# Four sequences instead of two in the loop of each engine: expert MLP, layer norm and rotation over 128 sequences

## The chip, the cores and the metric

The kernel runs on one core of one Trainium2 chip. Its time is the device time of one execution in microseconds (us). The core's engines each run a program of their own, and meet at semaphores: TensorE (PE in the profile; PEld is its loading of weights), VectorE (DVE), ScalarE (ACT), GpSimd (POOL) and SyncE (SP). DMA queues move data between memory and the core, and also bring the engines their instructions.

## The reference

There are 128 sequences of 128 tokens with 512 features. Each sequence names one of 8 experts; that expert's two-layer network, a residual, a layer norm and a rotation of groups of four features by the sequence's own two angles give the output.

```python
h = jax.nn.gelu(jnp.einsum('bsh,bhi->bsi', input_tensor, Wi_b) + bi_b[:, None, :], approximate=False)
o = jnp.einsum('bsi,bih->bsh', h, Wo_b) + bo_b[:, None, :]
r = o + input_tensor
mu = jnp.mean(r, axis=-1, keepdims=True)
var = jnp.mean(jnp.square(r - mu), axis=-1, keepdims=True)
y = (r - mu) * jax.lax.rsqrt(var + LN_EPS)
...
x0, x1, x2, x3 = (e[..., 0], e[..., 1], e[..., 2], e[..., 3])
out = jnp.stack([x0 * ct + x1 * st, -x0 * st + x1 * ct, x2 * cp + x3 * sp, -x2 * sp + x3 * cp], axis=-1)
```

Here `Wi_b`, `bi_b` and the others are the expert's arrays picked for each sequence, (512, 2048) and (2048, 512) for the two products; y is scaled by gamma and shifted by beta before the rotation, and ct, st, cp, sp are the cosines and sines of the sequence's theta and phi.

## The kernel before, in words

The sequences are sorted by expert at the start, on the chip; a table `tab` in SBUF says for each place s in that order which sequence it is, the rank of its expert among those used, and which of two weight buffers holds that expert. Weights and activations are split into a high and a low f16 part, and a product is made of three f16 products (`PASSES`), so that each of the two matrix products takes 4 groups (one for each PSUM bank of 512 columns) of 12 matmuls of 128x128 by 512 columns: 96 matmuls for a sequence.

All engines walk through the same places s. In its iteration s TensorE alternates between a group of the first product of s (`first_product`, L834, into `z_ps`) and a group of the second product of s-1 (`second_product`, L850, into `o_ps`). VectorE scales and adds the bias (`z_bank`, L647), ScalarE takes the gelu and the high part, VectorE takes the low part (`lo_group`, L657), SP transposes both parts by DMA into `hT16` (L257), which the second product of the next iteration reads. VectorE also prepares the input of s+1 (`scale_x`, `lo_x`) and does the residual, the layer norm and the rotation of s-2. GpSimd loads and splits the weights of the next expert, written out for each of the seven later experts and not in a loop. The places of a DMA queue and the order on each engine are the order in which the code is written.

What the change touches is `pipeline`. It gives each of TensorE, VectorE, ScalarE and SP the same schedule: iterations 1 and 2 written out, a loop on the engine itself (`Fori`) whose body holds two iterations and runs for i = 1 to 61 (s = 3 to 124), and the last five (s = 125 to 129, of which the last two only finish earlier sequences) written out. Inside the loop s is a number in a register. At the start of an iteration TensorE reads four entries of `tab` into registers (`slot_value`, L196, an instruction TENSOR_LOAD each, with register arithmetic), checks its semaphores, and only then passes on the first matmul; register and branch instructions run on the engine's sequencer, ahead of the matmuls that it has queued.

Of the kernel before, what the change touches and what calls it, by code (L numbers as in the profile page):

```python
# [67 lines left out]
def expert_mlp_rotate_kernel(nc, x, itok, theta, phi, Wi, bi, Wo, bo, gamma, beta, out):  # L68
    S, T, H = x.shape
# [11 lines left out]
    with ctx:  # L81
# [116 lines left out]
        def pipeline(engine, iteration):  # L198


            iteration(1, 1)
            iteration(2, 0)
            with engine.Fori(1, (S - 4) // 2) as i:
                iteration(i * 2 + 1, 1, True)
                iteration(i * 2 + 2, 0, True)
            for s in range(S - 3, S + 2):
                iteration(s, s % 2)

        def there(s, d, inner):
# [22 lines left out]
        def _(sp):  # L232
# [36 lines left out]
            iteration(-1, 1)  # L269
            iteration(0, 0)  # L270
            pipeline(sp, iteration)


# [165 lines left out]
        def _(act):  # L439
# [120 lines left out]
            hi_parts(1)  # L560

            pipeline(act, iteration)
            store(S - 1)
            act.wait_ge(s_y, 16 * S)
# [3 lines left out]
        def _(dve):  # L568
# [227 lines left out]
            lo_parts(1)  # L796

            pipeline(dve, iteration)


# [111 lines left out]
```

## Time and profile before

| | us |
|---|---|
| three runs | 2800.49, 2804.8, 2823.32 |
| their median | 2804.8 |
| the profiled execution: its time | 2803.09 |
| its span, first to last instruction | 2801.4 |
| TensorE busy in the span | 2684.1 |

The profiled execution lies 1.7 us below the median of the three, and its span 1.7 us below its own time. The granted clock of TensorE is 0.991 of full speed over the span.

### The profile page before, as it was taken

The page shows a single profiled execution, that of the slowest core. Times are in us where ns is not written, and L with a number is a line of the kernel's source. Part 1 is how long each engine was busy: PE and PEld are TensorE (multiplying, and loading weights), DVE is VectorE, ACT ScalarE, POOL GpSimd, SP SyncE. Part 2 cuts the span into 40 slices and gives each one's busy share as a digit, 9 for nine tenths or more (in the row PEclk, how much of TensorE's full clock was granted, in tenths as well). Part 3 has the DMA queues.
Part 4 walks back from the last instruction along what each step waited for, and adds up shares of the span by engine and source line. Part 5 has one row for each costly group of instructions (what it writes and reads, how often), then busy time and mean ns, then how long its engine had stood idle before and what let it go on. Part 6 is the DMA issues. An engine that isn't in the chain of part 4 may idle for free.

```text
span 2801.4 us, 55611 instructions
## 1 busy us (share of the span) xinstructions
PE 2684.1 (96%) x12306; PEld 1208.4 (43%) x12307; DVE 1956.2 (70%) x4919; ACT 931.1 (33%) x1689; POOL 1369.6 (49%) x1619
## 2 busy tenths in 40 slices
PE   2899999999999999999999999999999999999998
PEld 1344444444444444444444444444444444444443
DVE  4576677667777767777777776777777776777676
ACT  4333333333333333333333333333333333333332
POOL 4778617871007872478600478606873577500000
PEclk9899999999999999999999999999999999999999
DMA  4658556765436665657544658546675658444343
GB/s 159 150 132 195 118 136 148 182 144 122 86 82 167 173 148 126 147 130 186 139 98 88 147 131 180 141 98 157 159 162 132 165 131 168 113 91 89 82 97 65
DMA packets 742561, 375.90 MB, mean 134 GB/s; under 512 B 682816, under 2 KB 682944, under 8 KB 733824
## 3 DMA queue, kind: packets, MB, share of 16 engines
q1 hardware_dynamic: 677568, 173.95, 34.9%
q0 software_dynamic: 25984, 130.29, 14.7%
q10 hardware_dynamic: 38976, 71.32, 7.8%
q14 instruction: 25, 0.20, 0.0%
q8 instruction: 8, 0.13, 0.0%
HBM read 174.13 MB, written 33.55 MB: 74 GB/s over the span
## 4 chain that ended last, share of the span: by engine, by line
PE 78%; DMA 6%; DVE 6%; issue 5%; DVEq 2%; POOL 2%; ACT 1%; ACTq 0%; SPq 0%; POOLq 0%
PE z_ps L834 39%; PE o_ps L850 39%; DMA xT<-x 3%; DMA hT<-h 2%; DVE z_ps L647 1%; DVEq L196 1%; DMA xbuf<-in_x 1%; ACT z_ps L472 1%; DVE h L657 0%; ACT x L467 0%; DVE y L702 0%; POOL wo L340 0%; ACTq L196 0%; DVE ln L674 0%; DVE r_ps L673 0%
## 5 line engine op out<-in xcount | busy, mean ns | idle before, releaser
L834 PE MATMUL z_ps<-wi,xT 128*128 x6096 | 1407.2, 381 | 45.0 <-issue 21.7
L850 PE MATMUL o_ps<-wo,hT 128*128 x6144 | 1415.7, 380 | 17.2 <-DMA hT<-h 9.2
L834 PEld LDWEIGHTS z_ps<-wi,xT 128*128 128x128 f16 x6096 | 598.0, 98 | 781.4 <-issue 89.0
L850 PEld LDWEIGHTS o_ps<-wo,hT 128*128 128x128 f16 x6144 | 602.6, 98 | 748.4 <-issue 29.0
L472 ACT ACTIVATE z_ps<-z_ps 128x512 f32<-128x512 f32 x512 | 299.3, 585 | 1777.7 <-DVE z_ps L647 1763.4
L647 DVE SCALAR_TENSOR_TENSOR z_ps<-z_ps,tok,bi_all 128x512 f32<-128x512 f32 x512 | 387.5, 757 | 203.6 <-PE z_ps L834 144.5
L406 POOL TENSOR_TENSOR wi<-staged 128x512 f32<-128x512 f32 x112 | 117.1, 1046 | 658.3 <-DVE r_ps L667 647.2
L657 DVE SCALAR_TENSOR_TENSOR h<-z_ps,tok,h 128x512 f16<-128x512 f32 x512 | 380.6, 743 | 2.5 <-ACT h L478 1.6
L478 ACT ACTIVATE h<-z_ps,tok 128x512 f16<-128x512 f32 x512 | 352.4, 688 | 21.9 <-DMA hT<-h 0.4
L652 DVE SCALAR_TENSOR_TENSOR x<-xbuf,tok,x 128x512 f16<-128x512 f16 (+1 forms) x128 | 115.7, 904 | 192.2 <-ACT x L467 192.2
L702 DVE SCALAR_TENSOR_TENSOR y<-r_ps,rot,y 128x128 f32<-128x128 f32 x512 | 194.5, 455 | 5.8 <-ACT y L485 2.6
L339 POOL TENSOR_SCALAR staged<-staged,wscale 128x512 f32<-128x512 f32 x224 | 158.4, 707 | 20.9
L340 POOL TENSOR_TENSOR wo<-staged,wo 128x512 f16<-128x512 f32 x112 | 130.7, 1167 | 9.3
L340 POOL TENSOR_TENSOR wi<-staged,wi 128x512 f16<-128x512 f32 x112 | 130.0, 1160 | 9.3
L666 DVE TENSOR_SCALAR ln<-inv,ex 128x1 f32 (+1 forms) x128 | 27.4, 214 | 148.1 <-issue 140.7
L406 POOL TENSOR_TENSOR wo<-staged 128x512 f32<-128x512 f32 x112 | 117.3, 1047 | 7.4
L485 ACT ACTIVATE y<-r_ps,rot 128x256 f32<-128x256 f32 x256 | 109.4, 487 | 17.0 <-DVE r_ps L693 17.0
L408 POOL TENSOR_TENSOR wi<-wi 128x512 f32<-128x512 f32 x84 | 108.6, 1293 | 6.6
L408 POOL TENSOR_TENSOR wo<-wo 128x512 f32<-128x512 f32 x84 | 108.5, 1291 | 6.6
L667 DVE SCALAR_TENSOR_TENSOR r_ps<-o_ps,ln,xbuf 128x512 f32<-128x512 f32 x128 | 97.1, 759 | 19.2 <-DVE ln L666 18.8
L693 DVE SCALAR_TENSOR_TENSOR r_ps<-r_ps,ln,bgb_all 128x512 f32<-128x512 f32 x128 | 97.2, 759 | 18.3
L691 DVE SCALAR_TENSOR_TENSOR r_ps<-r_ps,ln,bgb_all 128x512 f32<-128x512 f32 x128 | 97.1, 759 | 18.2
(126 smaller groups left out, 1407.8 us busy)
## 6 DMA issues: line engine op xcount, KB each, us to landing
staged<-in_L_cond_Wi POOLq DMA_DIRECT2D x56, 1024.0 KB, 5.9
staged<-in_L_cond_Wo POOLq DMA_DIRECT2D x56, 1024.0 KB, 6.7
xbuf<-in_x ACTq DMA_DIRECT2D x128, 256.0 KB, 3.6
out<-y ACTq DMA_DIRECT2D x128, 256.0 KB, 3.4
hT<-h SPq DMA_TRANSPOSE x512, 3.9
bi_all<-in_L_cond_bi POOLq DMA_DIRECT2D x7, 1024.0 KB, 9.4
wi<-in_L_cond_Wi SPq DMA_DIRECT2D x4, 1024.0 KB, 8.5
wo<-in_L_cond_Wo ACTq DMA_DIRECT2D x4, 1024.0 KB, 11.5
```

Of the source, the lines that this page charges most:

```text
L339: chain.step(g.tensor_scalar(raw, raw, scale, 1.0, ALU.mult, ALU.mult))
L340: chain.step(g.tensor_tensor(lo, raw, hi, ALU.subtract))
L406: chain.step(g.tensor_tensor(to, raw[:, p], raw[:, p], ALU.mult))
L408: chain.step(g.tensor_tensor(acc[:, p], acc[:, p], sq[:, p], ALU.add))
L472: a.activation(bank, bank, ACT.Gelu).then_inc(s_gelu, 1)
L478: a.activation(h16[:, n, 0, :], bank, ACT.Copy, scale=HSCALE[k]).then_inc(s_hhi, 1)
L647: v.scalar_tensor_tensor(out=z_ps[:, n, :], in0=z_ps[:, n, :], scalar=ZS, in1=row(bi_all, b, hb), op0=ALU.mult, op1=ALU.add).then_inc(s_z, 1)
L652: v.scalar_tensor_tensor(out=x16[:, 1, :], in0=row(xbuf, s % XB), scalar=SX, in1=x16[:, 0, :], op0=ALU.mult, op1=ALU.subtract).then_inc(s_ ...
L657: v.scalar_tensor_tensor(out=h16[:, n, 1, :], in0=z_ps[:, n, :], scalar=HSCALE[k], in1=h16[:, n, 0, :], op0=ALU.mult, op1=ALU.subtract).th ...
L702: last = v.scalar_tensor_tensor(out=every(y[:], to), in0=every(r_ps[:], of), scalar=row(rot, s, slice(sine, sine + 1)), in1=every(y[:], to ...
L834: last = t.matmul(z_ps[:, n, :], xT16[:, j, a, k, :], wi16[:, bass.ds(b, 1), w, k, cs], start=(k == 0 and (a, w) == PASSES[0]), stop=(k == ...
L850: last = t.matmul(o_ps[:, j, :], hT16[:, n, a, c, :], wo16[:, bass.ds(b, 1), w, n * GC + c, :], start=(n == 0 and c == 0 and (a, w) == PAS ...
```

## The change

The loop's body holds four iterations instead of two and runs 30 times (s = 3 to 122); seven iterations (s = 123 to 129) are written out behind it instead of five. The first two iterations, the work of each iteration and the start of the kernel stay as they are. GpSimd's program is the same instruction by instruction.

```diff
             iteration(1, 1)
             iteration(2, 0)
-            with engine.Fori(1, (S - 4) // 2) as i:
-                iteration(i * 2 + 1, 1, True)
-                iteration(i * 2 + 2, 0, True)
-            for s in range(S - 3, S + 2):
+            with engine.Fori(0, (S - 8) // 4) as i:
+                for j in range(4):
+                    iteration(i * 4 + (3 + j), (1 + j) % 2, True)
+            for s in range(3 + (S - 8) // 4 * 4, S + 2):
                 iteration(s, s % 2)
```

On TensorE, behind the second iteration of the body, the kernel before has the loop's counter and its branch (L203). The branch goes back to the body's first TENSOR_LOAD; what is listed behind it is the first iteration after the loop.

```order
L850 ISA
L850 MATMUL o_ps<-wo,hT 128x512 x2
L203 REGISTER_ALU
L203 COMPARE_AND_BRANCH
L196 TENSOR_LOAD tab
L196 ISA x2
```

At the same place the changed kernel goes on with the third iteration's table reads.

```order
L850 ISA
L850 MATMUL o_ps<-wo,hT 128x512 x2
L196 TENSOR_LOAD tab
L196 ISA x2
L196 TENSOR_LOAD tab
L196 ISA x3
```

So the counter and the branch stand here no longer; they come once behind the fourth iteration. The listing of TensorE's program grows from 1058 rows to 1620.

On VectorE the same place in the kernel before is behind the last instruction of the rotation (L702); L64 clears the semaphore of VectorE's own steps.

```order
L702 SCALAR_TENSOR_TENSOR y<-r_ps,rot,y 128x128
L203 REGISTER_ALU
L203 COMPARE_AND_BRANCH
L64 ISA
L196 TENSOR_LOAD tab
L196 ISA x2
```

In the changed kernel:

```order
L702 SCALAR_TENSOR_TENSOR y<-r_ps,rot,y 128x128
L64 ISA
L196 ISA
L196 TENSOR_LOAD tab
L196 ISA x3
```

Here too the branch has moved behind the fourth iteration. VectorE's listing grows from 551 rows to 821, SP's from 105 to 145, GpSimd's stays at 1696.

## Rows read from the trace of the kernel before

**Rows 1.** The page, part 1: busy time of the engines.
```profile
PE 2684.1 (96%) x12306; PEld 1208.4 (43%) x12307; DVE 1956.2 (70%) x4919; ACT 931.1 (33%) x1689; POOL 1369.6 (49%) x1619
```

**Rows 2.** Chain that ended last, 2500 to 2640: start, us, what.
```profile
2507.62 0.21 issue
2507.83 2.76 PE z_ps L834 x12
...
2528.72 2.59 PE z_ps L834 x12
...
2549.44 0.21 issue
2549.65 2.76 PE z_ps L834 x12
```

**Rows 3.** The same chain in the written-out end, 2690 to 2802.
```profile
2716.75 2.59 PE z_ps L834 x12
...
2737.47 2.59 PE z_ps L834 x12
```

**Rows 4.** Waits of PE: total us, times, longest.
```profile
PE z_ps L834 <- issue: 21.7, 45, 2.7
PE z_ps L834 <- DMA xT<-x: 21.2, 6, 14.3
...
PE o_ps L850 <- DMA hT<-h: 9.2, 6, 3.4
```

**Rows 5.** The chain: the five long pieces of "issue" before PE, 255 to 2337.
```profile
255.85 2.54 issue
...
979.11 2.58 issue
...
1719.70 2.29 issue
...
2038.24 2.15 issue
...
2336.23 2.71 issue
```

**Rows 6.** All DMA queues, 200 to 2700: packets, MB, share of 16 engines.
```profile
q1 hardware_dynamic: 623040, 154.74, 35.4%
q0 software_dynamic: 24890, 122.25, 15.5%
q10 hardware_dynamic: 33984, 61.88, 7.7%
q14 instruction: 14, 0.11, 0.0%
```

**Rows 7.** DMA queue q8, 100 to 200, then 2717 to 2779.
```profile
q8 instruction: 4, 0.07, 0.3%
...
q8 instruction: 3, 0.05, 0.3%
```

**Rows 8.** Windows: 2717 to 2779: length, busy time of PE, PEld, DVE, ACT, POOL.
```profile
2717.00:2779.00 62.00, 62.00 (x289) 28.12 (x288) 43.01 (x111) 19.33 (x35) 0.00 (x0) 1.00 0.39 77
```

**Rows 9.** Timeline of DVE, 2569 to 2613: start, us, what, idle time before.
```profile
2588.82 0.76 DVE L647 SCALAR_TENSOR_TENSOR z_ps<-z_ps,tok,bi_all 128x512 f32<-128x512 f32 x1 [1.31 <-PE z_ps L834]
...
2596.82 0.74 DVE L657 SCALAR_TENSOR_TENSOR h<-z_ps,tok,h 128x512 f16<-128x512 f32 x1
...
2609.93 0.76 DVE L647 SCALAR_TENSOR_TENSOR z_ps<-z_ps,tok,bi_all 128x512 f32<-128x512 f32 x1 [1.58 <-PE z_ps L834]
```

**Rows 10.** The chain, 2300 to 2345: a wait at a change of expert.
```profile
2321.91 11.43 DMA hT<-h
...
2333.47 2.76 PE o_ps L850 x12
```

**Rows 11.** DMA issues: KB each, us from issue to landing.
```profile
hT<-in_itok_B SPq DMA_DIRECT2D x1, 64.0 KB, 3.1
...
hT<-in_condB_phi SPq DMA_DIRECT2D x1, 0.5 KB, 2.6
```

## The prediction

> **What bounds the kernel now.** I read the page's busy times first: TensorE is busy for 2684.1 of 2801.4 us, VectorE for 70% of the span, the others for half or less [rows 1]. So the question is what stands between TensorE's matmuls. The chain that ended last answers it in a quiet stretch, where no weights are being loaded: it is all TensorE, groups of 12 matmuls at 2.59 us, and a sequence of eight groups takes 8 x 2.59 = 20.72 us. Between the first and the second sequence of a loop body nothing is seen: from 2507.83 to the second sequence's first group at 2528.72 are 20.89 us, the eight groups and 0.17 us by which the first group (2.76) is longer than the rest. Behind the second sequence, where the loop jumps back, there are 0.21 us of "issue", and then again a first group of 2.76 [rows 2]. A pair takes 2549.65 - 2507.83 = 41.82 us against 2 x 20.72 = 41.44. In the written-out end of the program, which has no jump, the first groups lie 2737.47 - 2716.75 = 20.72 us apart and are no longer than the others [rows 3]. So a jump back costs TensorE 0.21 + 0.17 = 0.38 us, and a boundary that is written out costs nothing.
>
> The waits of TensorE say how often: 45 first-product instructions waited for "issue", 21.7 us in total [rows 4]. Five of these are long, 12.3 us together [rows 5]; they stand behind waits for a transposed activation, as at 2336.23, where the group before it had waited for a transpose of 11.43 us [rows 10]. The other 40 make 9.4 us, 0.24 each. With the 0.17 of the first group that is 0.41 us. The loop before jumps back 60 times (61 passes), so a third of the jumps cost nothing that shows: TensorE's sequencer was far enough ahead, or something else ended later.
>
> **The change part by part.** The loop of 30 passes jumps back 29 times, so 31 jumps go. Each removed jump becomes a boundary like the one inside the body before: the same four table reads, without counter and branch.
>
> If the removed jumps cost what the average one does, the gain is 31 x 40/60 x 0.41 = 8.5 us. A jump behind a drained queue costs too, though it is not among the 40: counting sequences along the chain, four of the five long pieces stand at jumps, 2.54, 2.58, 2.71 and 2.15, and one, 2.29, between the two sequences of a body [rows 5], so the jump adds some 0.3 there (2.15 ended in another kind of wait and is left out). Counting these four with the others, 31 x 44/60 x 0.41 = 9.3 us. That is the value I take. The upper bound is 31 x 0.41 = 12.7 us, if each removed jump costs what it does in a quiet stretch. The lower bound of this step is nothing, if TensorE then waits for the next in line: transposes of the activations.
>
> What is next in line in a quiet stretch? VectorE waits for TensorE once in each sequence, 1.31 and 1.58 us, before the fourth bank; the low part that closes a sequence is done at 2596.82 + 0.74 = 2597.56 [rows 9], and the group that needs its transpose is the last of the sequence in hand, which by the pattern of [rows 2] starts at 2549.65 + 41.82 + 20.89 - 2.59 = 2609.77. That is 12 us, of which the transpose takes some. So VectorE, ScalarE and SP follow a TensorE that is 0.2 us a sequence faster. Their own 31 jumps go as well, and are worth nothing, since none of them is on the path there.
>
> At changes of expert the weights that GpSimd fetches lengthen the transposes. There TensorE waits: 9.2 us for `hT`, 21.2 for `xT`, of which one wait of 14.3 is at the start [rows 4], and the 12.3 us of long pieces: 9.2 + 6.9 + 12.3 = 28 us in all. The change leaves these transfers and the order of the queues as they are, but shifts when they meet. I price that at nothing, with a quarter of the 28, 7 us, to either side.
>
> Written out in addition are two sequences at the end (123 and 124), with numbers known beforehand instead of registers: by [rows 3] these run at 20.72, which is nothing added. The two longest programs grow by half, and this is where the price could be: **the instructions must reach the engines.** Queue q8 brings them in packets of 0.05 / 3 = 17 KB. It brought three of them in the 62 us from 2717 to 2779, in which TensorE ran three written-out sequences [rows 7, 8]: about one packet for a sequence, and none of them stopped TensorE, which was busy all 62 us. I take q8 for TensorE's. From 100 to 200, when the sequences ahead of the loop and its first passes ran, came four [rows 7]; then, from 200 to 2700, not one [rows 6]. So a body of two sequences, some two to three packets, stays with the engine once loaded, and jumping back to its start asks for nothing. The other instruction queue, q14, serves the others in smaller packets (0.11 / 14 = 8 KB); its 14 packets in that stretch are two for each of the seven experts in GpSimd's written-out code, so VectorE's and ScalarE's bodies stay too. Whether a body of four sequences stays, four to five packets on TensorE, no row shows. From one side it costs nothing; from the other, a transfer at each of 29 jumps while the sequencer stands still. The nearest rows for one transfer's time are the small loads, 2.6 and 3.1 us from issue to landing [rows 11]; 29 x 2.6 to 3.1 is 75 to 90 us. Inside the body the fetch runs ahead, as in the written-out end, so the jump alone would pay. I take nothing, the side of [rows 6], which are the only ones that show jumps back over more code than one packet.
>
> The Trainium skill has a price for the jump itself: "Advanced Engine Details and Errata", section Control Flow Timing, gives about 108 ns for a compare-and-branch. By it 31 jumps would be an estimate of 3.3 us and the time 2800. The trace has more, since the table reads behind the jump come later too and the queue of matmuls runs dry.
>
> **The sum.** 2803.1 (the profiled execution) - 9.3 = 2793.8 us; the median of the three runs lies 1.7 above that execution. I predict 2794 us. The bounds: 2803.1 - 12.7 - 7 = 2783 and 2803.1 + 7 = 2810.
>
> **The rivals.**
>
> *TensorE's body no longer stays with the engine.* Each of 29 jumps waits for a packet with nothing in reserve, since the sequencer comes late there already [rows 2]: 75 to 90 us, less the 9.3, gives 2869 to 2884 us, slower by 2.4 to 2.9%. It decides from the point where the body of four and the packet fetched ahead of it exceed what the engine holds. For it speaks that only two sequences are shown to stay; against it that these stayed for 2500 us without a single packet, so that the store is not just two packets deep. The Trainium skill, "Runtime: NRT & Kernel Launch", section Instruction fetch mechanics, has a rule that makes this case: instructions lie in two blocks, and a taken branch to a target outside them waits for a fetch. By that rule the loop before should have fetched at its jumps as well, which [rows 6] do not show; the same section gives TensorE's store as 2048 instructions, in which the four sequences would fit.
>
> *VectorE's body no longer stays, TensorE's does.* VectorE then starts every fourth sequence some 3 us late. In quiet stretches the 12 us above, less a transpose, hide it. At changes of expert, where transposes take 11 us [rows 10], nothing hides it: the 6 + 6 waits and five long pieces [rows 4, 5] are some 12 places, and if half of them feel 3 us, 18 us come back: 2794 to 2812 us, no difference that can be told.
>
> *The whole path speeds up.* For 1% or more, 28 us, all jumps and most waits at the changes of expert would have to go; by a lucky shift of the transfers this gives 2775 us at best. Nothing in the profile points there.
>
> That the loop is not what it says can be left out: the listing shows the branch behind the fourth sequence.
>
> **How the numbers follow.** About 1% is what a measurement of this kernel can tell from no change. The forecast, 2783 to 2803, has 0.68; VectorE's late start, or the transfers meeting worse, 2803 to 2812, 0.15; TensorE's refetch, about 2876, 0.13; the large gain 0.04. The range 2784 to 2811 holds the first two less their ends, 8 in 10. Faster by over 1%: 0.04. Slower by over 1%: 0.14, the refetch and 0.01 for changes of expert that go badly wrong. Within 1%: 0.82.
>
> **What would show it.** In quiet stretches four sequences should take 4 x 20.72 + 0.38 = 83.26 us, with one piece of "issue" where there were two; waits of TensorE for "issue" should number some 25 instead of 45. Queue q8 should again bring nothing from 200 to 2700, and six or so packets in place of four before that. I am wrong if q8 shows tens of packets and pieces of "issue" of 2 to 3 us stand at each fourth sequence; if q14 does so without q8, the second rival holds; and if the pieces of "issue" are fewer and the time is no shorter, TensorE's waits for `hT` and `xT` have taken the gain.

## The result and the profile after

The changed kernel takes 2789.2 us (median of 20 runs, 2775.2 to 2801.9), the one before in runs beside it 2806.4 (20 runs, 2793.7 to 2823.3). The ratio, with its 95% interval, is 0.9938 [0.9923, 0.9954]: 17 us less, between 13 and 22. Predicted were 2794 us and a gain of 9.3. The range held, the size of the gain did not: nearly twice as much, and the experiments below show that TensorE's own jumps, from which the 9.3 were worked out, carry the smaller part of it.

The profiled execution took 2791.90 us. First the page's busy times, which answer to [rows 1]:

```profile
PE 2679.8 (96%) x12306; PEld 1208.7 (43%) x12307; DVE 1959.2 (70%) x4919; ACT 930.0 (33%) x1689; POOL 1368.4 (49%) x1619
```

TensorE does the same matmuls and is busy 4.3 us less. Most of it can be first groups that are no longer stretched: 21 waits for "issue" fewer (below) at 0.17 us make an estimate of 3.6. Next the chain that ended last, 2490 to 2640 (start, us, what), against [rows 2]:

```profile
2497.45 0.30 issue
2497.74 2.76 PE z_ps L834 x12
...
2580.80 0.27 issue
2581.07 2.76 PE z_ps L834 x12
```

Four sequences take 2581.07 - 2497.74 = 83.33 us, with one piece of "issue" in front (predicted: 83.26). TensorE's waits (us in all, times, longest), against [rows 4]; `xT` is the transposed input that the first product needs, `hT` the transposed activation of the second:

```profile
PE z_ps L834 <- DMA xT<-x: 18.8, 6, 13.9
PE o_ps L850 <- DMA hT<-h: 15.7, 6, 4.9
...
PE z_ps L834 <- issue: 11.5, 24, 2.5
```

"Issue" went from 45 waits to 24, from 21.7 us to 11.5. `xT` is shorter by 2.4 us, but `hT` took 6.5 more. And the queues that bring instructions, 100 to 200 and then 210 to 2660 (packets, MB, share of 16 engines), against [rows 6, 7]:

```profile
q8 instruction: 5, 0.08, 0.4%
```

```profile
q1 hardware_dynamic: 613028, 152.25, 36.8%
q0 software_dynamic: 24832, 121.91, 15.7%
q10 hardware_dynamic: 33552, 61.09, 8.0%
q14 instruction: 14, 0.11, 0.0%
```

Nothing from q8 in the loop: the body of four sequences stays with TensorE, and neither of the refetch rivals happened.

So the signs that were foretold are there, with five packets of q8 from 100 to 200 us in place of four, where six or so had been expected. Is the step behind them right too? In this pair of executions "issue" gave back 10.2 us and TensorE's busy time 4.3, more than 9.3, and then 6.5 were lost on `hT`. If the other engines followed TensorE as the prediction had it, `hT` should not have grown.

### The profile page after: what moved, and what is told of

Same layout as the page of the kernel before. It is cut to its first block, busy times and chain, and to the rows that moved or that the text cites. A ratio compares the mean times of both kernels' runs of the same rounds, so it can differ in the third digit from the quotient of the medians.

```text
span 2790.2 us, 54938 instructions
## 1 busy us (share of the span) xinstructions
PE 2679.8 (96%) x12306; PEld 1208.7 (43%) x12307; DVE 1959.2 (70%) x4919; ACT 930.0 (33%) x1689; POOL 1368.4 (49%) x1619
## 4 chain that ended last, share of the span: by engine, by line
PE 79%; DMA 6%; DVE 5%; issue 4%; POOL 2%; DVEq 2%; ACT 1%; ACTq 0%; SPq 0%; POOLq 0%
PE o_ps L850 40%; PE z_ps L834 39%; DMA hT<-h 2%; DMA xT<-x 2%; DMA xbuf<-in_x 2%; DVE z_ps L647 1%; DVEq L196 1%; ACT z_ps L472 1%; DVE h L657 0%; ACT x L467 0%; DVE ln L674 0%; DVE y L702 0%; DVE r_ps L673 0%; ACTq L196 0%; POOL wo L340 0%
## 5 line engine op out<-in xcount | busy, mean ns | idle before, releaser
L850 PE MATMUL o_ps<-wo,hT 128*128 x6144 | 1419.7, 381 | 24.0 <-DMA hT<-h 15.7
L702 DVE SCALAR_TENSOR_TENSOR y<-r_ps,rot,y 128x128 f32<-128x128 f32 x512 | 195.2, 456 | 5.0 <-ACT y L485 2.0
L667 DVE SCALAR_TENSOR_TENSOR r_ps<-o_ps,ln,xbuf 128x512 f32<-128x512 f32 x128 | 97.1, 759 | 15.4 <-DVE ln L666 13.9
```

What stands on the lines that cost most here:

```text
L702: last = v.scalar_tensor_tensor(out=every(y[:], to), in0=every(r_ps[:], of), scalar=row(rot, s, slice(sine, sine + 1)), in1=every(y[:], to ...
L850: last = t.matmul(o_ps[:, j, :], hT16[:, n, a, c, :], wo16[:, bass.ds(b, 1), w, n * GC + c, :], start=(n == 0 and c == 0 and (a, w) == PAS ...
```

## The experiments

Two theories. **A**, the prediction's: TensorE's jumps are the gain, the others' jumps are hidden. **D**: VectorE's own cycle is hardly shorter than TensorE's. When something at a change of expert has made it late, it catches up slowly or not at all, until a transpose of what it finished late stops TensorE; what its iteration costs in jumps and table reads then counts. In the expectations B is D's forerunner (the jumps of VectorE and ScalarE make the chain late at changes of expert), C says that the transfers there only happen to meet otherwise, and E that ScalarE's or SP's jump is the late one. All gains and losses below are the ratio to the kernel before, run beside, with its 95% interval, times that kernel's median (2801 to 2807 us).

**One engine's loop at a time.** `pipeline` gets a number of sequences for each engine:

```diff
+        BODY = {'sp': 2, 'act': 2, 'dve': 2, 'pe': 4}
...
-            with engine.Fori(1, (S - 4) // 2) as i:
-                iteration(i * 2 + 1, 1, True)
-                iteration(i * 2 + 2, 0, True)
-            for s in range(S - 3, S + 2):
+            n = BODY[name]
+            with engine.Fori(0, (S - 8) // n) as i:
+                for j in range(n):
+                    iteration(i * n + (3 + j), (1 + j) % 2, True)
+            for s in range(3 + (S - 8) // n * n, S + 2):
                 iteration(s, s % 2)
```

e1_pe4, four on TensorE alone.

> Only TensorE's loop holds four sequences; VectorE, ScalarE and SP keep two. Theory A (the gain is TensorE's own: its sequencer comes late at its jumps): all of the change's gain, 2789 us where the kernel before has 2806, that is 12 to 22 us faster, and waits of TensorE for issue fall from 45 to about 25. Theory B (the jumps of VectorE and ScalarE made the chain late at changes of expert): a gain of 5 us or less. Theory C (the transfers at changes of expert only happen to meet otherwise): anything between -8 and +8 us in the waits for hT and xT, with the issue part of 9 to 11 us beside it.

Measured: 2800.2 us, ratio 0.9981 [0.9966, 0.9996], a gain of 5 us (1 to 10). TensorE's waits in it:

```profile
PE o_ps L852 <- DMA hT<-h: 19.9, 9, 4.3
...
PE z_ps L836 <- issue: 15.8, 23, 2.8
```

Half the jumps are gone, as in the changed kernel (23 waits for "issue"), but `hT` takes 19.9 us instead of 9.2. Two thirds of the gain are missing.

e2_rest4, four on SP, ScalarE and VectorE, two on TensorE.

> The other half: VectorE, ScalarE and SP hold four sequences, TensorE keeps two. Theory A: no change, within 4 us of the kernel before, and 45 waits for issue again. Theory B: most of the 17 us. If both halves gain some 8 us each, the two theories share it.

Measured: 2792.5 us, ratio 0.9960 [0.9939, 0.9980], a gain of 11 us (6 to 17). Theory A had nothing for this.

```profile
PE z_ps L836 <- issue: 17.9, 42, 2.7
...
PE o_ps L852 <- DMA hT<-h: 4.6, 2, 2.6
```

TensorE's jumps are all there (42 waits), and the gain comes nonetheless, with two waits for `hT` instead of six. The two parts add up to the whole: 5 + 11 = 16 of 17 us. Theory A had 12 to 22 us for the first and nothing for the second, and falls.

**TensorE's gaps taken away without the loop.** e3_late_reads: the kernel before, but TensorE reads the two table entries that only the second product needs after it has passed on the first group of the first product, so that the sequencer is not late behind a jump.

```diff
-                if back:
-                    b1 = slot_value(pe, BUF, s - 1, 1)
-                    if not boot:
-                        r1 = slot_value(pe, RANK, s - 1, E - 1)
...
                     if here:
                         first_product(s, k, n, b)
+                    if n == 0 and back:
+                        b1 = slot_value(pe, BUF, s - 1, 1)
+                        if not boot:
+                            r1 = slot_value(pe, RANK, s - 1, E - 1)
```

> All loops hold two sequences as before. In TensorE's iteration the two table reads that only the second product needs are moved behind the first group of matmuls, so the sequencer has two reads (some 1.5 us) less to do between the last group of one sequence and the first of the next. Theory A: the jumps then cost nothing, 60 of them instead of the 31 that the change removes, so at least the change's 17 us and up to 35; pieces of issue of 0.2 us vanish, and those of 2.1 to 2.7 us behind a drained queue shrink by some 1.5 us. Theories B and C: no more than 5 us, since no jump is removed.

Measured: 2803.8 us, ratio 1.0002 [0.9983, 1.0021]: nothing (a gain of 5 to a loss of 6), where theory A had 17 us at least. Its waits:

```profile
PE o_ps L850 <- DMA hT<-h: 32.3, 13, 5.0
...
PE z_ps L834 <- issue: 1.4, 3, 0.6
```

The "issue" is gone, 20.3 us of it, and 23.1 us more of `hT` stand in its place: 13 waits instead of 6. This is the clearest case of a gain given back. That TensorE runs faster between the transposes and so meets the next one earlier is how I read it; the trace shows that VectorE is late more often, as counted below.

**VectorE's side.** Where the path leaves TensorE in the kernel before, it runs through VectorE for whole sequences; the chain that ended last, 1330 to 1440 (a wider stretch than any shown so far; DVEq is VectorE's sequencer, L196 the table read):

```profile
1341.32 0.70 DVEq L196
...
1347.03 0.77 DVE z_ps L647
...
1362.85 0.30 DVEq L196
...
1368.10 0.77 DVE z_ps L647
...
1383.37 0.73 DVEq L196
...
1389.11 0.77 DVE z_ps L647
...
1392.82 11.75 DMA xT<-x
1404.56 0.33 issue
1404.89 2.76 PE z_ps L834 x12
```

The first z bank of three sequences in a row lies on the chain: VectorE needs 1389.11 - 1347.03 = 42.08 us for two sequences, where TensorE needs 41.82 with a jump and 41.44 without one. Here it doesn't catch up; the input that it prepares late goes through its transpose, and TensorE waits. No matmul of TensorE lies on the chain in these 42.08 us: 26.4 are VectorE and its sequencer, 6.4 ScalarE and its sequencer, whose results VectorE waits for, and 9.3 "issue". So what is called VectorE's cycle is an iteration of VectorE with the steps of ScalarE inside it.

e5_dve4 has four on VectorE alone, e6_act4 on ScalarE alone (`dve` or `act` 4 in the `BODY` line of the first diff, 2 for the others).

> Only VectorE's loop holds four sequences, the others two. Theory D (VectorE, once a transfer has made it late, runs a cycle hardly shorter than TensorE's, so what its jumps take is what it lacks to catch up, and TensorE pays later in waits for transposes): most of the 14 us that the three engines together gave, that is 7 to 14 us faster than before, with waits for issue as before (about 45). Theory E (ScalarE's or SP's jump is the late one): 3 us or less.

> Only ScalarE's loop holds four sequences. Theory D: 0 to 4 us faster. Theory E: 7 us or more.

Measured: VectorE 2799.5 us, ratio 0.9969 [0.9948, 0.9989], a gain of 9 us (3 to 15). ScalarE 2799.8 us, ratio 0.9985 [0.9965, 1.0004], a gain of 4 us, which can't be told from nothing (a loss of 1 to a gain of 10). That is inside what theory D had for both, but the two medians are only 0.4 us apart and the two intervals overlap, so the pair doesn't tell VectorE's loop from ScalarE's. The profiled execution of e5 took 2808.7 us, 9 more than its median, and has 18.6 us of `hT`; its waits say nothing for D, only its time does.

e7_dve_one_read leaves all loops at two and takes away one of VectorE's three table reads in an iteration. The buffer of an expert is its rank modulo 2, so one entry gives both.

```diff
-                    b, r = slot_value(dve, BUF, s, 1), slot_value(dve, RANK, s, E - 1)
+                    r = slot_value(dve, RANK, s, E - 1)
+                    b = r % 2
```

> Loops of two as before. VectorE works out which weight buffer a sequence has from its expert's rank (r % 2, a register operation), and no longer reads it from the table: one read of three less in each of its iterations. No jump goes. Theory D: VectorE's cycle is shorter by some 0.4 us in every sequence, more than its jumps cost (0.26 us in every second), so at least 7 us and up to 25 us faster than before, and fewer sequences in which VectorE starts the first bank over 3.6 us after TensorE finished it (21 in the profile before). Theory A: no change, within 4 us.

Measured: 2794.6 us, ratio 0.9958 [0.9939, 0.9977], a gain of 12 us (6 to 17), with not one jump removed.

```profile
PE z_ps L835 <- issue: 18.2, 50, 3.2
...
PE o_ps L851 <- DMA hT<-h: 0.3, 1, 0.3
```

TensorE's jumps cost about what they did before; its waits for `hT` are gone. The sequences with a late VectorE, counted as in the expectation (first bank begun over 3.6 us after TensorE finished it), are 2 instead of 21.

e9_dve_extra_read goes the other way: the changed kernel, with one more table read in VectorE's iteration, whose value nobody uses.

```diff
                     b, r = slot_value(dve, BUF, s, 1), slot_value(dve, RANK, s, E - 1)
+                    slot_value(dve, RANK, s, E - 1)
```

> The changed kernel with one table read more, of no use, at the start of each of VectorE's iterations (the opposite of the run with one read less). TensorE's program is that of the changed kernel. Theory D: VectorE's cycle is some 0.4 to 0.7 us longer, so the change's gain is lost, 2800 to 2825 us against 2789, and the sequences with a late VectorE are well over the 13 of the changed kernel. Theory A: within 4 us of the changed kernel.

Measured: 2838.8 us, ratio 1.0132 [1.0111, 1.0153] to the kernel before, 37 us slower (31 to 43), and some 50 slower than the changed kernel: more than the 2800 to 2825 us that were expected. 98 sequences have a late VectorE, against 13 in the changed kernel. In e3 they are 34. (These are counts of one execution each; e1 and e6, which leave VectorE's loop alone, have 15 and 9, so a difference of ten or so from 21 says little.) The page's shares of the chain by engine, of before, of the changed kernel, of e7 and of e9 in this order:

```profile
PE 78%; DMA 6%; DVE 6%; issue 5%; DVEq 2%; POOL 2%; ACT 1%; ACTq 0%; SPq 0%; POOLq 0%
```

```profile
PE 79%; DMA 6%; DVE 5%; issue 4%; POOL 2%; DVEq 2%; ACT 1%; ACTq 0%; SPq 0%; POOLq 0%
```

```profile
PE 86%; DMA 4%; issue 3%; DVE 3%; POOL 2%; DVEq 1%; ACT 1%; ACTq 0%; SPq 0%; POOLq 0%
```

```profile
PE 39%; DVE 24%; issue 13%; DVEq 9%; ACT 6%; DMA 5%; POOL 2%; ACTq 1%; SPq 0%; POOLq 0%
```

One table read more in each iteration of VectorE (a load, its address arithmetic and a check of the value), and the chain lies on TensorE for 39% of the span only. In e9's chain, 1430 to 1525, the first z banks of five sequences follow each other:

```profile
1435.93 0.77 DVE z_ps L647
...
1457.43 0.77 DVE z_ps L647
...
1478.47 0.77 DVE z_ps L647
...
1499.43 0.77 DVE z_ps L647
...
1521.22 0.77 DVE z_ps L647
```

Four sequences take VectorE 85.29 us here, against TensorE's 83.33: in this stretch VectorE is the bound. The same row of VectorE's waits for TensorE, before, after, e7 and e9, shows how little lies between these cases:

```profile
DVE z_ps L647 <- PE z_ps L834: 144.5, 114, 3.8
```

```profile
DVE z_ps L647 <- PE z_ps L834: 156.8, 111, 3.8
```

```profile
DVE z_ps L647 <- PE z_ps L835: 183.6, 131, 3.8
```

```profile
DVE z_ps L647 <- PE z_ps L835: 47.4, 41, 3.8
```

VectorE's reserve, its wait for TensorE, is 144.5 us over 128 sequences before, 1.1 us each. In the changed kernel it is there in 111 sequences, with a read more in 41: the read took it for over half of all sequences.

**Both sides at once.** e10_fewer_reads: loops of two, VectorE as in e7, and TensorE reads only the ranks (two reads in an iteration instead of four).

```diff
-                    b1 = slot_value(pe, BUF, s - 1, 1)
-                    if not boot:
+                    if boot:
+                        b1 = slot_value(pe, BUF, s - 1, 1)
+                    else:
                         r1 = slot_value(pe, RANK, s - 1, E - 1)
+                        b1 = r1 % 2
                 if here:
-                    b, r = slot_value(pe, BUF, s, 1), slot_value(pe, RANK, s, E - 1)
+                    r = slot_value(pe, RANK, s, E - 1)
+                    b = r % 2
```

> Loops of two. Both TensorE (two reads instead of four) and VectorE (two instead of three) work out the weight buffer from the rank. TensorE's jumps then cost nothing, as in the run with late reads, which gained nothing by it; VectorE's cycle is that of the run with one read less, which gained 11 us. Theory D: now TensorE's part pays too, since VectorE can follow, 20 to 30 us faster than before, more than the two runs' gains together. If the two parts only add up: 8 to 14 us.

Measured: 2764.1 us, ratio 0.9873 [0.9851, 0.9896], 36 us less (29 to 42), more than the 20 to 30 expected and far more than the 8 to 14 of parts that only add up.

```profile
PE o_ps L851 <- DMA hT<-h: 6.2, 4, 2.6
...
PE z_ps L835 <- issue: 1.8, 3, 0.9
```

TensorE's gaps alone gave 0 (e3), VectorE's read alone 12 (e7); together they give 36. With VectorE on time, what TensorE gains stays. One part of this comparison is not clean: e3 moves TensorE's two reads and e10 drops them, and dropping them on TensorE alone was not run. Of the 43.8 us between the profiled spans of before and e10, 27.0 are waits for "issue", `xT` and `hT`, and 15.7 TensorE's busy time (2668.4 against 2684.1 us), of which more below.

e4_no_loop writes out all iterations on all four engines.

```diff
-            with engine.Fori(1, (S - 4) // 2) as i:
-                iteration(i * 2 + 1, 1, True)
-                iteration(i * 2 + 2, 0, True)
+            for s in range(3, S - 3):
+                iteration(s, s % 2, True)
```

> No loop on any engine: all 130 iterations are written out, with numbers instead of registers; every instruction is fetched once. Theory A with instructions fetched ahead in time: all 60 jumps gone, twice the change's gain, 2765 to 2785 us. If fetching straight code costs TensorE something, time is lost in pieces of issue at every packet of q8: about 140 packets, slower than the kernel before if each costs over 0.2 us.

Measured: 2763.5 us, ratio 0.9843 [0.9813, 0.9873], 44 us less (36 to 52). The instruction queue of TensorE over the whole run:

```profile
q8 instruction: 136, 2.23, 0.3%
```

That is about one packet for a sequence, and "issue" is 1.8 us in one wait, so fetching code that runs straight on costs nothing that shows, as [rows 7, 8] had it. The jumps are not all that is gone: without a register for s the arithmetic on it goes too (the page counts 51151 instructions against 55611), and VectorE's wait for TensorE rises from 144.5 to 245.9 us.

e12_no_loop_fewer_reads joins e4 and e10.

> No loop on any engine, and the fewer reads of both TensorE and VectorE: what the experiments point to. VectorE's cycle without loops is already short enough to follow, so the reads can bring only a little of the 20 us that remain in waits at changes of expert: 2745 to 2765 us, at least as fast as the run with no loop (2763.5).

Measured: 2756.3 us, ratio 0.9847 [0.9821, 0.9873], 43 us less (36 to 50). Not to be told from e4: with "issue" at 0.9 us and `hT` at 2.5 little is left for either edit to give. e4 and e12 are the fastest kernels of the study; e10, with a loop of two, comes close, its interval overlapping both of theirs.

**Where the rivals begin.** e8_all8 has eight sequences in every loop (15 passes), e11_pe8 in TensorE's alone.

> All loops hold eight sequences, 15 passes. By the jumps that go (45 instead of 31) some 20 to 28 us faster than the kernel before, if the eight sequences stay with the engines. If TensorE's body (about nine packets of q8) no longer stays: a burst of q8 packets in every pass, and at each of 14 jumps a wait of 2.6 us or more, 36 us and more lost, so slower than or equal to the kernel before. If only VectorE's body no longer stays: q14 shows tens of packets more, and the time is 2780 to 2800 us.

> Only TensorE's loop holds eight sequences, the others two. If the 58 us that eight sequences on all engines lost are TensorE's fetches at its 14 jumps: slower than before by 50 to 80 us, q8 with some ten packets in each pass and q14 with only the 14 of GpSimd. If VectorE's fetches had a part in it: 30 us or less.

Measured: 2864.3 us, ratio 1.0208 [1.0179, 1.0237], and 2864.4 us, ratio 1.0215 [1.0191, 1.0239]: 58 and 60 us slower. Instruction queues from 200 to 2600, of e8 and then of e11:

```profile
q8 instruction: 152, 2.49, 0.4%
q14 instruction: 180, 1.47, 0.2%
```

```profile
q8 instruction: 152, 2.49, 0.4%
q14 instruction: 14, 0.11, 0.0%
```

And e11's chain at two of its jumps:

```profile
2214.41 3.45 issue
2217.86 2.76 PE z_ps L842 x12
...
2567.80 4.07 issue
2571.86 5.30 PE z_ps L842 x12
2577.16 2.98 PE o_ps L858 x12
```

With eight the first rival is there: 152 packets in 14 passes, eleven for a pass. The second jump costs 4.07 us of "issue", 2.71 in the first group and 0.39 in the next, 7.2 us; the first one costs 3.45 and 0.17. What differs is the granted clock of TensorE, here of the two first groups (start:end, length and busy times as in [rows 8], then the clock, the DMA share and GB/s):

```profile
2217.90:2220.60 2.70, 2.70 (x13) 1.32 (x14) 0.77 (x5) 0.00 (x0) 0.00 (x0) 1.00 0.02 6
2571.86:2577.16 5.30, 5.30 (x13) 2.01 (x14) 1.82 (x7) 0.00 (x0) 0.00 (x0) 0.50 0.02 3
```

Behind the wait of 4.07 us TensorE ran at 0.50, the lower of its two levels (1.2 GHz), behind the one of 3.45 at full speed. At 13 of e11's 14 jumps the first group takes 4.1 us or more. All 14 waits together are 63.9 us, 3.4 to 8.8 each. Of the 65.4 us between the profiled spans of before and e11, "issue" makes 47.8 (69.5 us in 18 waits against 21.7) and TensorE's busy time 15.4 (2699.5 against 2684.1). In e8 "issue" is 79.0 us in 19 waits. The engines on q14 refetch in e8 alone (180 packets against 14), and that costs nothing that shows beside e11: 58 against 60 us. VectorE still waits 191.9 us for TensorE in e8, so there is room to hide it; what the longer loops of these engines would have given stands against it and isn't told apart.

The clock is at work in the kernel before, too; this is the chain at the long piece of [rows 5] that stands between the two sequences of a body:

```profile
1719.70 2.29 issue
1721.99 4.45 PE z_ps L834 x12
```

The granted clock was 0.51 from 1722.00 to 1725.40, and the group took 1.9 us more than 2.59. So a long wait can cost TensorE more than its own length, though not each one does (the 3.45 us in e11 did not), and what decides it isn't shown here. A kernel with few waits, as e10, has few groups at the lower clock and few stretched ones; its TensorE is busy for less.

## Why the prediction was right, and where it was not

**The jump itself** was sized well in a quiet stretch: 83.33 us for four sequences against 83.26, 24 waits for "issue" against about 25. In the whole pair the 10.2 us of waits and 4.3 of busy time are 14.5, above the 9.3 taken and above the upper bound of 12.7, and not all of it is jumps: the long waits for "issue" went from five, 12.8 us together by the idle times of the timeline, to three, 5.9 (2.51, 1.67 and 1.75). The prediction had counted those among the waits at changes of expert. It also left out that TensorE ran at the lower clock behind some of them (a group of 4.45 us behind the 2.29 above), where it had 0.17 for a first group.

**"Their own 31 jumps go as well, and are worth nothing"** is the step that failed. The 12 us between VectorE's last low part and its reader were read in one quiet stretch [rows 9], at a VectorE that was on time. There the reserve is real. In the stretch of 1330 to 1440, where GpSimd works on the next expert's weights (busy for 37.5 of the 42.08 us), VectorE is behind and has no reserve at all, and what decides is not how far its result is ahead of its reader elsewhere but how its cycle compares with TensorE's: 42.08 against 41.82 us, not shorter at all. The other engines' loops were worth 11 us (e2); e5 and e6 don't tell how much of it is VectorE's. So that the measured 2789 us lie inside the range is in part luck: the step that was to give 9.3 us gives about 5 (e1), and the larger part came from a step put at nothing.

**"TensorE then waits for the next in line"** stood in the prediction as the lower bound, nothing, and is what TensorE's loop by itself nearly gives: 5 us (e1), and 0 where the gaps go altogether (e3). So the term of 9.3 was near the price of the jumps and wrong as the gain from them. It was in part paid back in waits for `hT`, and the total of 17 us came out larger since the jumps of VectorE, ScalarE and SP went at the same time.

**Changes of expert at nothing, 7 us to either side**: the sign of the two waits there was mixed, `hT` + 6.5 and `xT` - 2.4 us; with the long waits, 6.9 us less, the three of them moved by some 3 us in all, inside the 7.

**The refetch of TensorE** was a sound mechanism at the wrong size, and not reached by four sequences. Eight show its price: 58 or 60 us and the gain forgone over 14 jumps, above 4 us each; the waits are 3.4 to 8.8 us, where 2.6 to 3.1 had been taken from a single small load, and behind 13 of the 14 a lengthened first group comes on top. The Trainium skill, "Runtime: NRT & Kernel Launch", section Instruction fetch mechanics, states both a store of 128 KiB for TensorE and a window of two blocks outside which a taken branch must fetch. The store agrees with the runs as far as they go: q8 brings 2.23 MB for 128 sequences (e4), 17 KB each, so by this estimate four sequences are some 70 KB and stay, eight some 139 KB and don't. The window of two does not agree: four such sequences, over four packets of 2.49 MB / 152 = 16 KB, stay for 2450 us without a fetch. **The refetch of VectorE** doesn't happen with a body of four (q14 brings the same 14 packets). With eight it costs nothing that shows where TensorE refetches too; eight on VectorE alone was not run.

What stays open: what two reads fewer give on TensorE alone, how many sequences between four and eight TensorE can hold (six was not run), how VectorE, ScalarE and SP share the 11 us (e5 and e6 overlap, and SP's loop alone was not tried), why e5's profiled execution is that far above its median, which waits are followed by the lower clock, and why the waits at changes of expert differ from kernel to kernel by more than the edits explain. That VectorE's cycle sets the time is shown by e7 and e9, which change nothing else, and by their counts of late sequences, 2 and 98; that the four-sequence loop helps by the same way is argued from e2, e5 and the counts of 21 before and 13 after, not shown.

## What to carry to other kernels

An engine with 70% busy time can be next to the bound: compare the length of its iteration when it is late, sequencer work included, with that of the bounding engine, not its distance in a quiet stretch. Before removing gaps on the bounding engine, look for the transfers that would then be waited for, and shorten the engine ahead of these first; here 0 and 12 us apart became 36 together. A longer loop body paid here with four sequences, where it stayed with the engine, and cost with eight, where it did not; the queue that brings instructions shows which side one is on.

## What the runs showed of the hardware

A table read into a register is not cheap, and not always the same: on VectorE's sequencer, before, 382 of them took 298 ns at least, 310 at the median and 1114 at most, and in the stretch shown above one took 0.70 and 0.73 us in two sequences and 0.30 in the one between. Two fewer on TensorE and one fewer on VectorE saved more than all jumps that the change removes (36 against 17 us). The Trainium skill, "Runtime: NRT & Kernel Launch", section Instruction fetch mechanics, gives some 200 ns a register for TENSOR_LOAD, with the loads of the program's preamble in mind; the reads of this table in SBUF took longer. Why some take twice the time of the others is not shown.

A jump to code that must be fetched cost TensorE a wait of 3.4 us or more in e11, and often a slow first group behind it. That the slow group belongs to the clock and not to the fetch is seen from two places: the jump at 2214.41 fetched and its group took 2.76 us at a granted clock of 1.00, and the group of 4.45 us in the kernel before ran at 0.51 behind a wait without any fetch.
